# Attention's weighing: the weighed rows laid out in runs of four features, four instructions a tile

## The reference, cut to what matters

```python
e = a_src[:, src] + a_dst[:, dst] + fc_b[0]
e = jax.nn.leaky_relu(e, negative_slope=0.2)
seg_max = jax.ops.segment_max(e.T, src, num_segments=n)
e = jnp.exp(e - seg_max.T[:, src])
seg_sum = jax.ops.segment_sum(e.T, src, num_segments=n)
att = e / seg_sum.T[:, src]
msg = att[:, :, None] * hp[:, dst, :]
agg = jax.vmap(lambda m: jax.ops.segment_sum(m, src, num_segments=n))(msg)
out = agg.mean(axis=0) + bias
```

## Time and profile before

| | us |
|---|---|
| median of 3 runs (26022.92 to 26029.44) | 26026.72 |
| the profiled execution, its own time | 26033.88 |
| its span in the trace | 26032.1 |
| first to last start of the reduction of `weighed` (147 of them) | 16056.9 to 17526.8 |
| VectorE busy in the whole span | 15740.5 (60%) |
| GpSimd busy in the whole span | 14448.5 (56%) |
| TensorE busy in the whole span | 14761.0 (57%) |

### The profile page before, as it was taken

One profiled execution on the slowest core, in us unless ns is written; L12 is line 12 of the kernel. 1 busy time (PEld: TensorE's weight loads), 2 busy tenths in 40 slices (PEclk: granted clock), 3 DMA queues, 4 the chain that ended last, 5 costly groups with the idle time before them and its releaser, 6 DMA issues. The chain is left out here.

```text
span 26032.1 us, 473806 instructions
## 1 busy us (share of the span) xinstructions
PE 14761.0 (57%) x105565; PEld 9264.3 (36%) x105566; DVE 15740.5 (60%) x32221; ACT 5279.9 (20%) x13135; POOL 14448.5 (56%) x14298
## 2 busy tenths in 40 slices
PE   7555555567666679972000000005577777777777
PEld 5344444334333368851000000005233333333333
DVE  9666666665556654442111114995777777777777
ACT  4211111111111134421000000000222222222222
POOL 0377777677777744433777777760333333333333
PEclk9655555555555555555555555555899999999999
DMA  2466666533333345412333332221444544444454
GB/s 66 112 172 173 172 173 172 128 68 68 68 68 68 68 119 154 146 51 53 92 92 92 92 92 79 72 65 30 114 117 117 118 118 118 118 118 119 118 119 110
DMA packets 3004699, 2740.20 MB, mean 105 GB/s; under 512 B 1459983, under 2 KB 2366029, under 8 KB 3001618
## 3 DMA queue, kind: packets, MB, share of 16 engines
q1 hardware_dynamic: 2437198, 2308.99, 33.5%
q0 software_dynamic: 412544, 241.53, 6.4%
q10 hardware_dynamic: 153668, 172.93, 2.7%
HBM read 2173.27 MB, written 537.90 MB: 104 GB/s over the span
## 5 line engine op out<-in xcount | busy, mean ns | idle before, releaser
L2571 POOL DMA_INDIRECT rows_x<-x_table,index x3125 | 2961.4, 948 | 5359.1 <-DMA index<-in_src 4596.6
L742 POOL DMA_INDIRECT rows<-split_table,index x3125 | 2999.3, 960 | 1943.2 <-DMA index<-in_src 1008.4
L1624 POOL DMA_INDIRECT rows_dram<-rows,place_now x3125 | 3028.1, 969 | 1489.1 <-issue 951.9
L858 POOL DMA_INDIRECT rows<-x_table,index x3125 | 3282.0, 1050 | 1021.1 <-issue 951.8
L1552 DVE TENSOR_REDUCE rows<-banks 128x108 f32<-128x324 f32 x1250 | 490.3, 434 | 3468.9 <-DMA rows_dram<-rows,place_now 3452.6
L1564 PE MATMUL banks<-row_pieces,hot_turned 128*128 x3125 | 393.6, 290 | 3609.9 <-DMA hot_turned<-turned_dram 3606.6
L2278 DVE TENSOR_TENSOR first<-banks,h 128x768 f32<-128x768 f32 x2500 | 1940.0, 817 | 786.5 <-PE banks L2401 672.1
L2286 DVE TENSOR_TENSOR second<-banks,h 128x768 f32<-128x768 f32 x2500 | 1943.7, 819 | 620.1 <-PE banks L2425 604.1
L550 PE MATMUL banks<-counts,low_turned 128*128 128x98 f32 x6250 | 1783.2, 433 | 82.8 <-ACT counts L538 50.1
L550 PEld LDWEIGHTS banks<-counts,low_turned 128*128 128x128 f32 x6250 | 1591.6, 313 | 205.8 <-issue 175.9
L1564 PEld LDWEIGHTS banks<-row_pieces,hot_turned 128*128 128x128 bf16 x3125 | 251.0, 134 | 3752.5 <-issue 3752.5
(11 more groups left out here) (475 smaller groups left out, 33351.8 us busy)
## 6 DMA issues: line engine op xcount, KB each, us to landing
key_row<-dst_rows SPq DMA_DIRECT2D x1250, 320.0 KB, 3.5
h<-hidden_dram SPq DMA_DIRECT2D x10000, 40.0 KB
acc_moved<-dst_rows SPq DMA_DIRECT2D x625, 320.0 KB
src_row<-in_src_rows SPq DMA_DIRECT2D x625, 320.0 KB
hot_turned<-turned_dram SPq DMA_DIRECT2D x1250, 160.0 KB, 2.2
hot_dram<-onehot SPq DMA_DIRECT2D x625, 160.0 KB
turned_dram<-hot_turned SPq DMA_DIRECT2D x625, 160.0 KB
a_dram<-a ACTq DMA_DIRECT2D x625, 160.0 KB
```

Source lines behind the costliest of these rows:

```text
L742: nc.gpsimd.indirect_dma_start(out=m["rows"][j][:, t * SPLIT:(t + 1) * SPLIT], out_offset=None, in_=m["split_table"], in_offset=bass.Indir ...
L858: nc.gpsimd.indirect_dma_start(out=m["rows"][j][:, t * C2:t * C2 + F], out_offset=None, in_=m["x_table"], in_offset=bass.IndirectOffsetOnA ...
L1624: nc.gpsimd.indirect_dma_start(out=m["rows_dram"], out_offset=bass.IndirectOffsetOnAxis(ap=m["place_now"][j][:, t:t + 1], axis=0), in_=m[" ...
L2571: nc.gpsimd.indirect_dma_start(out=m["rows_x"][j][:, t * F:(t + 1) * F], out_offset=None, in_=m["x_table"], in_offset=bass.IndirectOffsetO ...
```

## The change

`weighed` keeps its size, but within a group v and a head its 512 products now lie as: block of four features (8), slot (16), feature in the block (4). `weigh` becomes four instructions of 512 elements, one for each head, on VectorE for group 1 and on GpSimd for group 0. Each reads runs of 4 neighbouring features, goes on to the next slot 36 elements further, and writes one element behind the other. The exponential is repeated for the four features of a run, and the next slot's lies 4 elements further. The semaphore is raised by the last of the four. The reduction over the slots still takes 4096 elements and writes the same 256 in the same order, but now reads elements that lie 4 elements, 16 bytes, apart. Nothing else changes.

```diff
@@ -1641,6 +1641,7 @@
+    QUAD = 4
     VS = VG * SPAN
     VH = VG * HEADS
@@ -1649,10 +1650,13 @@
-    def weigh(eng, j, first, last):
-        v, first, last = first // SPAN, first % SPAN, (last - 1) % SPAN + 1
-        return eng.tensor_tensor(m["weighed"][j][:, v * SPAN * HF:(v + 1) * SPAN * HF].rearrange("p (h f e) -> p e h f", h=HEADS, f=F)[:, first:last],
-                                 rep(of_tiles(j)[:, v, first:last, 0:F], 2, HEADS), rep(logits(j)[:, v, first:last], 3, F), ALU.mult)
+    def weigh(eng, j, v):
+        for h in range(HEADS):
+            at = (v * HEADS + h) * SPAN * F
+            ins = eng.tensor_tensor(m["weighed"][j][:, at:at + SPAN * F].rearrange("p (b e q) -> p b e q", e=SPAN, q=QUAD),
+                                    of_tiles(j)[:, v, :, 0:F].rearrange("p e (b q) -> p b e q", q=QUAD),
+                                    rep(rep(logits(j)[:, v, :, h], 1, F // QUAD), 3, QUAD), ALU.mult)
+        return ins
@@ -1681,13 +1685,13 @@
-        weigh(nc.vector, j, SPAN, VS).then_inc(s["weighed"], 1)
+        weigh(nc.vector, j, 1).then_inc(s["weighed"], 1)
...
-        nc.vector.tensor_reduce(m["vec"][j][:, :].rearrange("p (v w) -> p v w", v=VG),
-                                m["weighed"][j][:, :].rearrange("p (v w e) -> p v w e", v=VG, w=HF), AX.X, ALU.add).then_inc(s["summed"], 1)
+        nc.vector.tensor_reduce(m["vec"][j][:, :].rearrange("p (w q) -> p w q", q=QUAD),
+                                m["weighed"][j][:, :].rearrange("p (w e q) -> p w q e", e=SPAN, q=QUAD), AX.X, ALU.add).then_inc(s["summed"], 1)
@@ -1715,7 +1719,7 @@
-                weigh(nc.gpsimd, j, 0, SPAN).then_inc(s["pool_weighed"], 1)
+                weigh(nc.gpsimd, j, 0).then_inc(s["pool_weighed"], 1)
```

## The result

| | before | after |
|---|---|---|
| median of 4 runs, us | 26026.4 | 26547.6 (26542.9 to 26552.4) |
| ratio | | 1.020, 95% interval 1.0184 to 1.0216 |
| span of the profiled execution, us | 26032.1 | 26541.1 |
| the stage: 147 tiles, us each (first to last start of the long reduction) | 10.07 | 13.53 |

The change costs 521 us where 409 were forecast: slower, as forecast, and inside the range. The stage's pace is (18039.4 - 16063.5) / 146 = 13.53 us a tile, which is 509 us more for 147 tiles, and 509 us is also what the two spans differ by. So all of it lies in this stage.

The account below looks back on a forecast made before the run. VectorE's own sequence (busy 395.8 of 400 us) was taken to bound the stage. Products, reduction and vanished collision gave 11.05 us a tile for 10.07, +144 us; with waits between engines +409, hence 26436 us, range 26130 to 26600.

Parts of the forecast that it names:

- alternation: Products in 98 tiles: VectorE's second to fourth pieces each wait for one GpSimd piece; +265 us, kernel 26436 us, 50%.
- main case: The forecast with engines taking turns piece by piece: +409 us, 26436 us, own range 26210 to 26530, 50%.
- the rival at 26,583: Meeting products: GpSimd, once in, keeps VectorE out for its four pieces, 4.2 us in 98 tiles; 8%.
- (1): VectorE's product: four pieces writing neighbours take 2.43 us in place of 3.42, -0.99 us a tile.
- (2): Long reduction: elements 16 bytes apart cost 0.63 ns more each, 6.99 us, +2.58 us a tile.
- (3): GpSimd's product: four pieces of 1.09 us, 4.36 together (ends 0.91 and 1.23 each), hidden in GpSimd's idle time.
- (4): GpSimd's late product against VectorE's additions, one tile in three: collision goes, covered by the longer reduction, -0.62 us a tile.
- (5): Both engines' pieces meet in 98 of 147 tiles: three waits of about 0.9 us each, +265 us.
- no alternation: Rival: VectorE's four pieces leave no gap for GpSimd where products meet; +144 us, 26171 us, 23%.
- GpSimd keeps its place: Rival on meeting products: GpSimd, once in, holds VectorE out for all four pieces, 4.2 us in 98 tiles; 26583 us, 8%.
- free step of 16 bytes: Rival: long reduction stays at 4.41 us; alone -110 us, 25917 (10%); with engines taking turns +154, 26181 (7%).
- the pieces do nothing for VectorE: Rival: short runs cost as the wide writes did, VectorE's product 3.90 us for 2.43; 26652 us, 2%.

## Why the prediction came out right

The case with the highest chance, alternation, is what happened, with the sign, the place and the count: half of the 588 pieces are long, which is 3 x 98. The sizes did less well. The time lies 112 us above the forecast of 26,436, 18 above the main case's own range (it ended at 26,530), and 52 below the end of the full range, which reached that far to take in the rival at 26,583. Of the 112 us, 100 are the change's price (509 for 409) and 12 come from the profiled executions: the one of before lay 7 us above its median, which the forecast took off again, and the one of after lay 5 below its own. Term by term:

- **(1) VectorE's pieces**: 2.40 us where they are alone, 2.43 forecast. Short runs are free, as line 1665 had said.
- **(2) The reduction**: 7.33 us, 6.99 forecast. Line 1685 was the right row for the sign: its step of 16 bytes does pay. The price an element was 0.71 ns and not the 0.63 that I took from line 869; the other long row, line 1265, had 0.71, and was the stated end. This term was mis-sized by 0.34 x 147 = 50 us.
- **(3) GpSimd's pieces**: 1.25 us, 1.09 forecast, and just beyond the upper end of 1.23. The line through 320 and 2048 elements took the price to lie in the elements alone; the short runs add 1.8 ns each. By itself this was hidden, but it went into (5).
- **(4) The old collision**: gone, as said. Line 1669 has a mean of 0.23 us. The longer reduction covers it, and the run that read on brought it back. The margin was luck: in the late tile above VectorE asks 7.60 us after the start of the reduction and GpSimd lets go at 7.79, so they still touch (0.41 us for 0.34). Reduction and pieces were both longer than forecast, and the two errors nearly cancel here.
- **(5) The alternation**: three waits in each of 98 tiles, 1.06 us each where 0.9 was forecast, since a piece of GpSimd is longer: 0.48 x 98 = 47 us more. The rule that a piece delays by its length less 0.16 us held (1.25 less 0.19); the length in it, from (3), was wrong. The run without meetings gives 312 us for the whole term (265 forecast, 3.18 x 98 = 312).

409 + 50 + 47 = 506 of the 509 that the spans differ by.

Of the rivals, no alternation fell with the 1.67 us between VectorE's pieces. That GpSimd keeps its place for all four did not happen where the products meet, but it is what line 1669 met in the late tiles wherever the reduction was short: the first turn showed one product of GpSimd against short instructions, and could not tell one piece from four. The free step of 16 bytes, alone or with alternation, fell with the reduction; at 8 bytes it exists. That the pieces do nothing for VectorE fell with 2.40 us where it asked for 3.90.

## What to carry to other kernels

For VectorE, lay out fp32 data so that every 16 bytes are touched at least twice in a row: runs of two where products read, a step of two where a reduction reads. (Runs that start at an odd element, and writes in short runs, were not tried.) GpSimd is another matter: its pieces got longer with every halving of the runs. Before an instruction with two SBUF inputs is split on one engine, look whether the other engine runs such instructions at the same time. Here each seam between two pieces let the other in (no run keeps the new layout in one instruction, so this is read from the timeline and from VectorE's single product of before, which never waited). A semaphore that sends its work beside a one-input instruction takes that cost away (312 us here). And ask of each wait in the trace what covers it: here the longer reduction hid a collision that came back as soon as it was shortened.

## What the hardware showed that was not expected

- The step of 4 fp32 elements costs nearly as much as one of 8 (0.71 and 0.75 ns an element), the step of 2 nothing. Steps of 3 and of 5 to 7 were not tried.
- Where both inputs of a VectorE product step on with every element, the price is paid once (1040 ns for 677), not twice.
- Two series of two-input instructions take turns one for one. A piece of VectorE makes GpSimd wait 0.45 us, a piece of GpSimd makes VectorE wait 1.06, and no time is lost beyond that: 4 x 0.61 + 3 x 1.06 = 5.62 us, 5.61 measured. One line of VectorE was passed over at several change-overs of GpSimd's pieces, and no run here says why.
